# Two of three score columns in one 1024-column exponential, with the probabilities in a ring of twelve columns

## The reference, cut to what matters

```python
qkv = (x @ w_qkv.T + b_qkv).reshape(b, n, 3, H, D).transpose(2, 0, 3, 1, 4)   # b=4, n=1024, H=16, D=8
q, k, v = (qkv[0], qkv[1], qkv[2])
attn = jnp.einsum('bhnd,bhmd->bhnm', q, k) * SCALE
attn = jax.nn.softmax(attn, axis=-1)
out = jnp.einsum('bhnm,bhmd->bhnd', attn, v)
```

## Time and profile before

| | us |
|---|---|
| median of 3 runs | 2063.98 (2062.31 to 2080.03) |
| the profiled execution, its own time | 2064.81 |
| its span on the core | 2063.0 |
| TensorE busy | 1711.1 (83%) |
| VectorE busy | 1499.3 (73%) |
| ScalarE busy | 949.7 (46%) |
| GpSimd busy | 371.2 (18%) |
| mean granted TensorE clock, share of full | 0.92 |

### The profile page before, as it was taken

The page is one execution under the profiler, slowest core; times in us unless marked ns, Lnnn a source line. Parts: engine busy times, 40 slices in busy tenths (PEclk is TensorE's granted clock), DMA queues, the critical chain, the costliest instruction groups (busy, mean ns, idle before and its releaser), DMA issues.

```text
span 2063.0 us, 32223 instructions
## 1 busy us (share of the span) xinstructions
PE 1711.1 (83%) x10833; PEld 998.6 (48%) x10833; DVE 1499.3 (73%) x2526; ACT 949.7 (46%) x1803; POOL 371.2 (18%) x637
## 2 busy tenths in 40 slices
PE   4799999549999899999998669999976659885675
PEld 3688888301212112212221368888855545553454
DVE  5655555688999998999983456555669848886884
ACT  2222222607778787877877522222235412111452
POOL 5210010400000000000000220010025652333442
PEclk9999999858999999999999969999988769997787
DMA  3000000210000000000000000000000000000000
GB/s 113 1 1 0 0 0 1 102 52 24 25 17 17 17 23 27 17 17 17 22 12 1 9 38 1 0 0 0 0 1 0 1 0 2 1 0 1 1 20 21
DMA packets 23270, 30.95 MB, mean 15 GB/s; under 512 B 4928, under 2 KB 19072, under 8 KB 22656
## 3 DMA queue, kind: packets, MB, share of 16 engines
q1 hardware_dynamic: 23168, 29.59, 4.3%
HBM read 20.80 MB, written 8.39 MB: 14 GB/s over the span
## 4 chain that ended last, share of the span: by engine, by line
PE 58%; DVE 21%; issue 8%; ACT 6%; POOL 5%; DMA 1%; DVEq 1%; POOLq 1%; SPq 0%; ACTq 0%
PE PS L313 11%; PE PS L738 9%; DVE neg_half L832 7%; PE PS L726 6%; PE PS L302 6%; PE PS L303 6%; PE PS L304 6%; PE PS L715 3%; ACT probs L800 3%; DVE shared L1550 3%; DVE qk_all L1085 3%; PE PS L1303 2%; PE PS L1415 1%; DVE qk_all L1088 1%; ACT qk_all L1081 1%
## 5 line engine op out<-in xcount | busy, mean ns | idle before, releaser
L832 DVE TENSOR_REDUCE neg_half<-PS 128x2 f32<-128x1024 f32 x512 | 599.6, 1219 | 52.6 <-PE PS L715 41.7
L800 ACT ACTIVATE probs<-PS 128x512 f32<-128x512 f32 x1024 | 537.2, 603 | 197.3 <-PE PS L726 197.0
L364 ACT ACTIVATE shared<-PS 128x512 f32<-128x512 f32 x256 | 153.1, 598 | 427.0 <-PE PS L304 411.0
L478 DVE TENSOR_TENSOR shared<-shared,PS 128x512 f32<-128x512 f32 x256 | 175.7, 687 | 175.1 <-ACT shared L364 174.7
L738 PE MATMUL PS<-probs,Vg 128*32 128x512 f32 x2048 | 275.8, 610 | 21.2 <-ACT OTs L808 21.1
L726 PE MATMUL PS<-qk_all 51*128 51x512 bf16 x1024 | 261.8, 388 | 13.5 <-ACT probs L800 10.4
L715 PE MATMUL PS<-qk_all 48*128 48x512 bf16 x1024 | 199.6, 401 | 71.9 <-DVE neg_half L832 39.0
L313 PEld LDWEIGHTS PS<-wd,shared 128*128 128x128 f32 x2048 | 247.9, 191 | 11.5
L313 PE MATMUL PS<-wd,shared 128*128 128x128 f32 x2048 | 248.6, 275 | 0.0
L726 PEld LDWEIGHTS PS<-qk_all 51*128 51x128 bf16 x1024 | 69.2, 93 | 311.2 <-ACT probs L800 289.2
L486 DVE SCALAR_TENSOR_TENSOR x<-PS,gates,x 128x128 f32 (+1 forms) x512 | 144.2, 344 | 71.9 <-PE PS L313 71.9
(11 more groups left out here) (200 smaller groups left out, 2339.6 us busy)
## 6 DMA issues: line engine op xcount, KB each, us to landing
split<-shared SPq DMA_DIRECT2D x16, 384.0 KB, 3.3
qk_all<-split SPq DMA_DIRECT2D x64, 96.0 KB
qk_all<-split SPq DMA_DIRECT2D x64, 64.0 KB
qk_all<-split SPq DMA_DIRECT2D x64, 32.0 KB
probs<-in_ret_const SPq DMA_DIRECT2D x1, 1538.5 KB, 6.6
qk_all<-negT SPq DMA_DIRECT2D x96, 4.0 KB, 1.8
probs<-in_w_gate SPq DMA_DIRECT2D x1, 1024.0 KB, 5.6
probs<-in_w_up SPq DMA_DIRECT2D x1, 1024.0 KB, 7.7
```

The lines of the kernel that those rows point to most:

```text
L364: act.activation(sg[:, f, :], bank(f), ACT.Silu).then_inc(s["silu"], 1)
L478: dve.tensor_tensor(h[:, FCH * (e % 2) + f, :], sg[:, f, :], bank(2 + f), ALU.mult).then_inc(s["h"], 1)
L800: act.activation(probs[:, n % 2, STRIPS * strip + pair, :], bank(RING_AT + use % RING), ACT.Exp, scale=ATT_SCALE).then_inc(s["exped"], 1)
L832: dve.tensor_reduce(neg_half[m % 2][:, :, at], bank(b, 2).rearrange("p (s w) -> p s w", s=STRIPS), AX.X, ALU.max, negate=True).then_inc(s[ ...
```

## The change

`probs` becomes one ring of twelve columns (three steps) in place of two sets of four. The place of a column is `use % 12`, so the columns lie in the order of their numbers. The exponentials no longer follow the steps. Where `use % 3 == 0`, one instruction of 1024 columns takes columns use and use + 1 from banks 4 and 5 and writes two neighbouring places; where `use % 3 == 2`, one instruction of 512 columns takes bank 6. A pair waits for both of its columns and raises `exped` by two when it ends. Each exponential also waits for the values that last read its place. The two copies of bank 7 are put in front of the first exponential that begins at the third column of the step (c), or behind a pair that began at b. TensorE's order, its waits in `scoreT` and `values` and the ring of three banks stay as they are. The other names that share the memory of `probs` (`wg_raw`, `wu_raw`, `qkf`, `rest`, `oT`, `biased`, `kconst`) are written anew for the same places.

```diff
+PROBS = 3 * JH
...
-        probs = sb("probs", [P, 2, JH, GW])
+        probs = sb("probs", [P, PROBS, GW])
...
-                    last = pe.matmul(bank(7)[j * 32:(j + 1) * 32, :], Vg[:, kt, j, :], probs[:, n % 2, j, :],
+                    last = pe.matmul(bank(7)[j * 32:(j + 1) * 32, :], Vg[:, kt, j, :], probs[:, (64 * r + 4 * n + STRIPS * (j % 2) + j // 2) % PROBS, :],
                                      start=(kt == 0), stop=(kt == BT - 1))
...
-            def exps(r, n, pair):
-                if pair == 0:
-                    wait(act, s["pv"], STEPS * r + n - 1)
-                for strip in range(STRIPS):
-                    use = 64 * r + 4 * n + STRIPS * pair + strip
-                    act.wait_ge(s["scoredT"], use + 1)
-                    act.activation(probs[:, n % 2, STRIPS * strip + pair, :], bank(RING_AT + use % RING), ACT.Exp,
-                                   scale=ATT_SCALE).then_inc(s["exped"], 1)
+            def exps(use, count):
+                wait(act, s["pv"], (use + count - 1 - PROBS) // 4 + 1)
+                act.wait_ge(s["scoredT"], use + count)
+                place = use % PROBS
+                act.activation(probs[:, place:place + count, :].rearrange("p j w -> p (j w)"), bank(RING_AT + use % RING, count),
+                               ACT.Exp, scale=ATT_SCALE).then_inc(s["exped"], count)
...
+            last = 64 * AG
+            for use in range(last):
+                at = use % 64
+                if at == 4 + 2 and use > 64:
+                    evacuate(use // 64 - 1, 1)
+                if at == 4 * (BT + 1) + 2:
+                    evacuate(use // 64, 0)
+                if use % RING == 0:
+                    exps(use, min(2, last - use))
+                elif use % RING == 2:
+                    exps(use, 1)
+            evacuate(AG - 1, 1)
```

More of the change, by code:

```diff
@@ L114, in macaron @@
         O = shared[:, :].rearrange("p (t g c) -> p t g c", t=TILES, g=HG)
-        probs = sb("probs", [P, 2, JH, GW])
[L117 to L120, removed]
+        probs = sb("probs", [P, PROBS, GW])
+        wg_raw, wu_raw = (probs[:, k * JH:(k + 1) * JH, :].rearrange("p j w -> p (j w)") for k in range(2))
+        qkf, rest = (probs[:, k * JH:(k + 1) * JH, :].rearrange("p (u k) w -> p u k w", u=2) for k in range(2))
+        oT = probs[:, 0:2, :]
         wqkv = sb("wqkv", [P, 3 * C])
@@ L175, in macaron @@
         pd = shared[:, 0:HG * JH * P].rearrange("p (g j l) -> p g j l", g=HG, j=JH)
-        kconst = probs[:, :, :, :].rearrange("p a j w -> p (a j w)")
+        kconst = probs[:, 0:2 * JH, :].rearrange("p j w -> p (j w)")
         at = [0]
@@ L952, in att_proj_dve @@
             s = att
-            biased = probs[:, 1, 0, :]
+            biased = probs[:, JH, :]
             def turn(g, u):
```

## The result

The changed kernel takes 2158.68 us (median of 4 runs, 2152.39 to 2161.86) against 2063.7 us for the kernel before in the same comparison: 1.0445 times as long, 95% interval 1.04 to 1.049. The profiled execution took 2159.29 us with a span of 2157.5 us, so this execution is 94.5 us longer than the one before. The forecast was 2129 us with a range of 2105 to 2160: the sign and the range hold, the point is 30 us too low.

The account below looks back on a forecast made before the run. A latency loop between TensorE and ScalarE, with no engine full, bounds the attention stage. Plain steps +74, copies +4, transposes -3 and negated maxima -11 sum to +64 us on 2064.8: 2129 us, range 2105 to 2160.

Parts of the forecast that it names:

- the loop: Attention stage: a step's first column, exponential, fourth column, values, next first column; 2.45 us (0.48, 0.60, 0.05, 0.32, 1.00).
- the plain steps: Attention steps without copy, transposes or negated maxima; 2.45 us before, forecast 2.87, 2.87 and 2.48.
- step A: First of three steps, columns 0 to 3, 0 and 1 paired; column 3 waits until 1.55; forecast 2.87 us.
- step C: Third of three steps, columns 8 to 11, 9 and 10 paired; forecast 2.48 us.
- Copies: Attention steps with a copy of bank 7: mean extra 0.87 us against 0.75, 31 copies, +4 us.
- Transposes: Steps at the output's transposes: 1.03 us stays, the next step's VectorE wait 0.20 against 0.38, 15 times, -3 us.
- Negated maxima: Steps stalled by VectorE's negated maxima: mean extra 0.3 us against 1.03, 15 times, -11 us.
- the rival that it falls: TensorE's clock falls at copies in the attention stage: +20 to +30 us, 2149 to 2159 us; chance 0.17.
- Two accesses: Exponential over two banks read as two accesses, taking up to 1.20 us: +40 us, 2170 us; chance 0.08.
- Cover better than walked: TensorE's waits in the attention stage better hidden: change costs +35 to +50 us, 2100 to 2115 us; chance 0.10.
- ScalarE's stream as the bound: ScalarE as full engine sets the attention step: 341 starts saved give -41 us, 2024 us; chance 0.05.
- pair 3+4: Joint exponential of columns 3 and 4, in the second of three steps, 0.48 to 1.50 us; ScalarE idle about 1.4 before.

Follow-up runs that it names:

- filler: The changed kernel with four additional score matmuls of 512 columns in each step of the last round, into banks 2 and 3, read by nobody: 2139.45 us.

## Why the prediction was right, and where it was not

**The range.** The sign, the loop and the plain steps came as forecast, but that 2158.68 us lies in 2105 to 2160 is in part luck: it is 1.3 us inside, one of the four runs (2161.86) is outside, and the upper end was drawn for a cost that hardly came. Of the 94.5 us the walk gave 64 and was 6 short; the short falls at copies, for which the upper end was drawn, gave 3.7; the long fall, which the prediction had not priced, gave 18.6. About 2 us stay unexplained.

**The bound and the pair.** The loop was read rightly from the earlier trace rows: with the pair at 1.024 us, the terms 0.05, 0.32 and 1.00 behind it are in the profile after unchanged. The estimate for a pair by the Trainium skill's formula (page "ScalarE: Activation LUTs", section "What ACT_TABLE_LOAD costs"), 1.04 us, was 0.015 above the trace; the slope from the earlier trace rows was nearer.

**The three steps.** Forecast 2.87, 2.87 and 2.48, measured 2.93, 2.90 and 2.45; 8.28 in place of 8.22. The mis-sized term is the start of a pair: 0.48 behind its column by the earlier trace rows, 0.54 in step A and 0.50 in step B. In step C it was the other way: column 10 came at 0.75, not 0.92, since the score tiles run beside column 9, and pair 9+10 ends before the next a is due. Together +5 us over the stage.

**The longer steps.** Copies: 0.26, 0.75 and 1.48 extra against 0.27, 0.74 and 1.60. Transposes: 1.02 in two kinds of round and 1.67 in the third (3.85 for a step of 2.45 and 3.20 for the next of 2.93), mean 1.24 against 1.23 forecast. Negated maxima: 0.65, 0.63 and 0 extra, mean 0.43; I had said 0.3, and before it was 1.03. So VectorE's stalls were hidden behind the pairs as forecast, a little less well. A round by the forecast's terms is 16 x 2.74 + 2 x 0.87 + 1.23 + 0.30 = 47.1 us; measured 47.3, 47.0 and 48.2 for the three kinds, mean 47.5. At full clock the forecast was 6 us short over the stage.

**The clock.** This is the step that failed. The likeliest case had the clock stay as it was, and the rival that it falls had 0.17. It fell, and the time is the rival's (2149 to 2159), but not by the rival's mechanism. That one had about ten short falls at copies in step C, at 2 to 3 us each. There are ten such steps, and three of them brought a fall, of 1.1 to 1.4 us. The price was made up by one fall that lasted 75 us through the last round. The prediction's argument against a fall, that the score tiles keep the clock up at a copy, did not hold either: the three short falls lie in rounds that have their tiles. The earlier trace rows allowed two readings. The fall there, at 1117.0 us, began 0.8 us behind the start of a copy, and also 16 us behind the last score tile (1100.7). The copy in the timeline of the kernel before:

```profile
1116.23 0.60 ACT L808 ACTIVATE OTs<-PS 128x512 f32<-128x512 f32 x1
```

I used the row to price the gaps and did not ask what longer steps do to the stretch without tiles. In the profiled executions the kernels whose plain steps are all 2.45 us have the clock low for 0 to 7 us there, and those with longer steps and no filler for 44 to 75 us. Why longer steps do this, no run shows.

**The rivals.** Two accesses: out, the pair takes 1.024 us and two single instructions are slower. Cover better than walked: out, plain steps came out longer, not shorter. ScalarE's stream as the bound: out; it saved 341 instructions and its idle time grew by 41 us. The rule of the Trainium skill quoted there (page "Perfetto Trace Analysis", section "Optimizing Scalar/DVE Operations"), that breaking instructions up can help where the engine is not full but keeps others waiting, agrees with the runs: 2064 us single and 2159 in pairs. The runs add the condition: the pairs that are not on the loop cost 18 us, those on it 77, with the long fall of the clock in it.

**The signs named beforehand.** 341 and 342 instructions: yes. ScalarE idle about 1.4 us before pair 3+4: 1.23 us at 1061.95 and 0.84 at 1053.66, where the step before was disturbed. VectorE's idle time in the stage was to rise by the same 64 us as the time; it rose by 94 (stage of 778.3 us with 574.9 busy, before 686.3 with 576.5), 63 of it before the maxima. So it rose with the time, as the sign says, but by the larger amount. Waits of line 726 for exponentials, in 400 us: 160.4 us in 149 steps before, 198.3 on the weight loads and 38.2 on matmuls in 134 steps now. That is 1.08 and 1.76 us a step: 0.7 more and not the 0.3 named, since waits that overlap other work are counted too. Of the signs of a wrong forecast one came true: the clock in the stage is 0.95.

## What to carry to other kernels

Where engines hand PSUM banks around a short ring, an instruction over several banks starts with its last input and frees its first bank with its last output; it can pay only if its engine is full and if the bank that the ring waits for next is not inside it. That it pays then is not shown: in every run here pairs cost time. Walk one common period of the ring and the issue order (here 3 banks and 4 columns, 12 columns) with starts from the trace; that gives which member of a pair is on the loop. Look then for copies that stand behind work they do not depend on, which gave the only gain here, and for the stretch in which the clock fell already before the change.

## What the runs showed of the hardware

One exponential of 1024 columns over two neighbouring PSUM banks takes 1.024 us, 0.43 more than one of 512 (0.595). The slope of line 1081 gives 0.42 for 512 more columns, so reading across the bank's edge costs nothing that shows.

Once at half clock, TensorE can stay there: in the last round of the changed kernel the matmul rows cover 61.60 of 76 us and the granted clock stays at 0.51, with steps of 3.75 to 4.24 us. With four more matmuls a step the clock came back and was at 0.98 over the last round, and the kernel was 19 us faster.

The three short falls in the middle of the stage each began within 1 us of the start of a copy in a step C. TensorE stood for 1.4 to 1.6 us at each of the ten copies of this kind, and seven of them brought no fall.
